# Cross-attention's key stack, written by half of the context: six transfers and two semaphores in place of three transfers and one

## The reference, cut to what matters

```
x   = layernorm(tgt);  self-attention (causal), result = tgt + sa_out
xq  = layernorm(result, ln2)            # 224 rows
xs  = layernorm(src, ln2)               # 750 rows of context
k2, v2 = split(xs @ ed_wkv);  q2 = xq @ ed_wq
wei2 = softmax(q2 @ k2^T * scale)       # per head 224 x 750
result = result + (wei2 @ v2) @ ed_wproj + ed_bproj
result = result + relu(layernorm(tgt, ln3) @ ff_w1 + ff_b1) @ ff_w2 + ff_b2
```

## Time and profile before

| | us |
|---|---|
| median of 3 runs | 1497.84 |
| lowest, highest | 1495.59, 1500.98 |
| the profiled execution's own time | 1497.26 |
| its span, first to last instruction | 1495.4 |
| span of the cross-attention, from 735 on | 760.4 |

### The profile page before, as it was taken

The page is one execution under the profiler, slowest core; times in us unless marked ns, Lnnn a source line. Parts: engine busy times, 40 slices in busy tenths (PEclk is TensorE's granted clock), DMA queues, the critical chain, the costliest instruction groups (busy, mean ns, idle before and its releaser), DMA issues.

```text
span 1495.4 us, 26115 instructions
## 1 busy us (share of the span) xinstructions
PE 1352.8 (90%) x9689; PEld 1113.9 (74%) x9689; DVE 826.8 (55%) x2056; ACT 667.8 (45%) x1622; POOL 654.1 (44%) x547
## 2 busy tenths in 40 slices
PE   6899999995999999998458899999989999999986
PEld 5699988984878888887347676777867677777853
DVE  4421222242477677788325767676675767666551
ACT  4322211241556666565023555463645546374431
POOL 3133322340444555553420455554554445555563
PEclk9999999997999999998768999999999999999996
DMA  5301110034636555654346765566647656665520
GB/s 172 131 22 43 42 42 21 28 129 132 120 68 146 147 131 125 150 122 141 95 80 83 122 89 106 84 103 117 86 91 106 111 85 107 103 94 72 93 36 26
DMA packets 97056, 142.13 MB, mean 95 GB/s; under 512 B 9521, under 2 KB 62553, under 8 KB 95945
## 3 DMA queue, kind: packets, MB, share of 16 engines
q1 hardware_dynamic: 96944, 140.67, 46.8%
HBM read 59.40 MB, written 22.02 MB: 54 GB/s over the span
## 4 chain that ended last, share of the span: by engine, by line
PE 35%; DMA 6%; DVE 4%; ACT 3%; POOL 1%; issue 1%; POOLq 0%; SPq 0%; ACTq 0%
PE ca_ps_acc L1411 16%; PE ca_ps_p L1428 5%; DMA ctx_tokens<-in_ctx_dram 5%; PE ca_ps_s L1441 5%; PE ca_ps_o L1455 5%; PE ca_ps_acc L1504 3%; DVE ca_xT L1394 2%; DVE ca_maxes L1360 1%; ACT ca_f L1329 1%; DMA ca_k_stack<-ca_keys 1%; ACT ca_xT L1323 1%; PE ca_ps_o L1470 1%; POOL ca_partial L1275 1%; ACT ca_probT L1296 1%; PE ca_ps_acc L1496 0%
## 5 line engine op out<-in xcount | busy, mean ns | idle before, releaser
L1275 POOL TENSOR_TENSOR ca_partial<-ca_partial,ca_probT 125x896 f32<-125x896 f32 x128 | 272.5, 2129 | 235.2 <-ACT ca_probT L1296 230.2
L1296 ACT ACTIVATE ca_probT<-ca_ps_p 125x448 f32<-125x448 f32 x384 | 209.8, 551 | 229.7 <-PE ca_ps_p L1428 228.4
L1360 DVE TENSOR_REDUCE ca_maxes<-ca_ps_s 112x1 f32<-112x375 f32 x512 | 253.2, 540 | 84.4 <-PE ca_ps_s L1441 83.8
L1441 PE MATMUL ca_ps_s<-ca_k_stack,ca_q_stack 96*112 96x376 f32 x512 | 173.5, 368 | 34.8 <-DVE ca_maxes L1360 20.8
L1428 PEld LDWEIGHTS ca_ps_p<-ca_q_stack,ca_k_stack 98*125 98x125 f32 x768 | 132.9, 191 | 53.3 <-issue 41.0
L402 PE MATMUL ff_ps_y<-ff_w,ff_hT 128*128 128x512 f32 x672 | 161.0, 396 | 6.7 <-DVE ff_w L63 6.7
L1428 PE MATMUL ca_ps_p<-ca_q_stack,ca_k_stack 98*125 98x224 f32 x768 | 163.4, 297 | 3.2 <-ACT ca_probT L1296 3.0
L1411 PE MATMUL ca_ps_acc<-ca_xT,w_a 128*128 128x376 f32 x768 | 158.9, 345 | 6.7 <-DVE ca_xT L1394 6.7
L262 POOL TENSOR_TENSOR ff_hT<-ff_hrelu,ff_hT 128x256 fp32r<-128x256 f32 x112 | 86.1, 771 | 162.3 <-DVE ff_hT L345 162.3
L1411 PE MATMUL ca_ps_acc<-w_b,ca_xT 128*125 128x512 f32 x576 | 152.5, 401 | 0.8 <-DVE ca_keys L1389 0.8
L402 PEld LDWEIGHTS ff_ps_y<-ff_w,ff_hT 128*128 128x128 f32 x672 | 126.3, 191 | 33.3 <-issue 4.2
(11 more groups left out here) (131 smaller groups left out, 2388.4 us busy)
## 6 DMA issues: line engine op xcount, KB each, us to landing
ca_k_stack<-ca_keys SPq DMA_DIRECT2D x96, 376.0 KB, 8.0
ctx_tokens<-in_ctx_dram SPq DMA_DIRECT2D x8, 1500.0 KB
sa_Q_stack<-sa_rows SPq DMA_DIRECT2D x96, 112.0 KB, 3.4
sa_K_stack<-sa_rows SPq DMA_DIRECT2D x96, 112.0 KB, 3.7
ca_q_stack<-q_out SPq DMA_DIRECT2D x96, 112.0 KB, 10.0
ctx_tokens<-in_L_xattn_ff_w_dram SPq DMA_DIRECT2D x16, 512.0 KB, 4.5
q_out<-sa_yT SPq DMA_DIRECT2D x16, 448.0 KB, 3.6
ff_xin<-in_x_dram SPq DMA_DIRECT2D x7, 512.0 KB, 3.8
```

The lines of the kernel that those rows point to most:

```text
L1275: pool.tensor_tensor(total, total, half(a), ALU.add).then_inc(partial_done, 1)
L1296: act.activation(probT[0:JT, step % PAIRS, u % GH].rearrange("p a t -> p (a t)"), ps_p[u % 2][0:JT, 0:2 * T], ACT.Exp).then_inc(exp_done, 1)
L1360: dve.tensor_reduce(maxes[:, q, j, a:a + 1], ps_s[n % 3][0:TQ, 0:JH], AX_X, ALU.max).then_inc(s_read, 1)
L1441: pe.matmul(ps_s[n % 3][0:TQ, 0:JP], q_stack[0:KS, h, TQ * q:TQ * (q + 1)], k_stack[0:KS, h, a, :], start=True, stop=True).then_inc(s_psum, 1)
```

## The change

The three transfers for a group become six, three for each half `a`. The three of half `a` are issued behind the `K_rest` of that half, and have a semaphore of their own. A piece is then 1,504 bytes, and again there are 128 of them in a transfer; the bytes in all are the same. TensorE waits for half 0 before the first score (which reads half 0) and for half 1 before the second; ACT waits for half `a` of the group before, ahead of writing half `a`. On SP the three transfers of half 0 now stand ahead of `queries` in the steps with `g` = 0, and ahead of `M` in the others.

```diff
-        k_stacked = [sem(f"k_stacked{g}") for g in range(KT)]
+        k_stacked = [[sem(f"k_stacked{g}_{a}") for a in range(2)] for g in range(KT)]
...
-                    if name == "K_rest" and item[2] == 1:
-                        G = item[1]
+                    if name == "K_rest":
+                        _, G, a = item
                         g = G % KT
-                        for a in range(2):
-                            wait_acc_read(sp, place["K", G, a])
+                        wait_acc_read(sp, place["K", G, a])
                         if G >= KT:
                             sp.wait_ge(p_psum, UNITS * (G - KT + 1))
                         for c, half in enumerate(STACK_K):
-                            sp.dma_start(k_stack[HD * c:HD * (c + 1), GH * g:GH * (g + 1)].bitcast(F32),
-                                         keys[:, half].bitcast(F32)).then_inc(k_stacked[g], 16)
+                            sp.dma_start(k_stack[HD * c:HD * (c + 1), GH * g:GH * (g + 1), a].bitcast(F32),
+                                         keys[:, half, a].bitcast(F32)).then_inc(k_stacked[g][a], 16)
...
-                        if a == 0 and G > 0:
-                            act.wait_ge(k_stacked[(G - 1) % KT], STACKED_K * ((G - 1) // KT + 1))
+                        if G > 0:
+                            act.wait_ge(k_stacked[(G - 1) % KT][a], STACKED_K * ((G - 1) // KT + 1))
                         act.copy(keys[:, HI, a], acc[:, 0:JP]).then_inc(khi_done, 1)
...
+                        if u < 2:
+                            pe.wait_ge(k_stacked[G % KT][a], STACKED_K * (G // KT + 1))
                         if u == 0:
-                            pe.wait_ge(k_stacked[G % KT], STACKED_K * (G // KT + 1))
                             pe.wait_ge(q_stacked[G % KT], STACKED_Q * (G // KT + 1))
```

## The result

The changed kernel takes 1526.74 us (median of 4 runs, 1525.16 to 1528.65) against 1499.03 (4 runs, 1495.59 to 1500.98): ratio 1.0188, 95% interval 1.0164 to 1.0211. It is slower by 28 us. The profiled execution took 1528.65 us, with a span of 1526.6, 31.2 us above the span of before. All ratios here are of fast executions; one of six_both_late's ten (1562.51 us) and one of held_both's ten (3283.01 us) were slow and do not enter them.

What follows compares the result with a forecast made beforehand. TensorE's work was taken to set the pace, with the context load's landing the deadline near the change. Profiled 1497.3 - 3 (beginning) + 27.5 (loads) + 9 (clock) = 1530.8, said as 1530 us, 2.2% slower; range 1496 to 1548.

Steps and rivals of the forecast that it cites:

- Fewer waits for the stack: Steady part: TensorE has no stack waits to lose and ACT catches up; 0, bounds 0 and -10.6 us.
- More issues and smaller pieces: SP's 96 more issues and the 1,504-byte pieces, all steps: 0 each; bounds for the issues 0 and +3 us.
- The load with half 0 in its flight: Steps with g = 0: early stack transfers delay the context load, 5 x 5.1 + 2 = 27.5 us, bounds 0 and 38.5.
- The clock: After longer TensorE stops at five loads the granted clock falls to 0.50: 5 x 1.8 = 9 us, bounds 0 and 18.
- The beginning: Phase's beginning: half 0 lands some 3 us earlier and the value product fits in; gain 3 us, bounds 0 and -6.2.
- the bytes to be moved are unchanged, so half 1 lands at about 787 again: Step at the phase's beginning: half 1 lands no sooner than the whole stack did, 787.02; only half 0 gains.
- A: Rival: stack uses the DMA engines the load leaves free, only the beginning's gain is left; 1494 us, chance 0.14.
- B: Rival: as A, and ACT's seven waits, 10.6 us, were passed on to TensorE by the banks; 1484 us, chance 0.11.

Runs made afterwards that it cites:

- six_both_late: Kernel before, with six transfers of 1,504-byte pieces and a semaphore for each half, none issued before both halves are split; 1492.51 us, ratio 0.9954.
- held_both: Changed kernel, but in the six steps with g = 0 and a context load in flight both halves wait for the second; 1496.47 us, ratio 0.9970.

## Why the prediction was right, by its own steps

The forecast was 1530.8 by the sum, 1530 as said, and 1526.74 was measured; the profiled execution, on which the sum was made, took 1528.65.

- *Fewer waits for the stack, 0:* right. Seven waits of ACT went, and the stretches of held_both are those of before.
- *More issues and smaller pieces, 0:* right that they cost nothing, by six_both_late. But they are not neutral at the beginning: there the six transfers bring the whole stack in 2.9 us sooner with nothing issued early.
- *The load with half 0 in its flight, 5.1 us at five places and 2 at the first:* right in mechanism, too large. The load's pieces grew by 4.4 us (15.4 to 19.8), and DVE's waits from 9.8 to 31.6 us over the five, 4.4 each. TensorE stood 21.5 us longer over the five, and the stretch behind the first load grew by 1.3: 22.8 in place of 27.5. The split was 2.5 and 1.9, where I had 3.4 and 1.7. I had taken half 0's price from the beginning of the kernel before, with pieces of double length. With the short pieces the whole stack costs the load 5.2 us there (20.3 in six_both_late against 15.1) and not 6.9, and half of that, 2.6, is close to what half 0 cost.
- *The clock, 1.8 us at five places:* right in mechanism, too small. TensorE's busy time for the same work grew by 13.5 us over the five, where I had 9. Behind the stop at 934 the half clock stood for all or most of 934 to 940, longer than in the one place of before from which I had the 1.8.
- *The beginning, -3:* the mis-sized term of the other sign, -5.9. The stop went down by 4.3 us, not 3, and the stretch up to the next load by another 1.6. The step that failed is "the bytes to be moved are unchanged, so half 1 lands at about 787 again": it was in place 25.4 us after the load's issue, not 28.1, as in six_both_late. Half 0, which I had at 784, was there by 782.39, and what the first score then waited for until 783.76 was the query stack, which I had counted as harmless behind half 0. This new wait, at the one place where the queries are read soon, cost up to 1.4 us.
- *Rivals A and B:* A (the load isn't disturbed) fell with the first load piece of 19 us, and B, whose gain was to come from ACT's seven waits, with the stretches of held_both, 85.3 us without them. The 435 GB/s ceiling that the Trainium skill gives ("DMA: Bandwidth & Descriptors", Specifications) is not contradicted: the wide load reached 258 GB/s. But with load and stack in flight most windows stay well below 200 GB/s, and what the ceiling leaves over did not keep the load from being slowed.

In sum: -5.9 for the beginning, 22.8 for the loads, 13.5 for the clock and 0.9 ahead of the first load make 31.3, against the 31.2 of the spans. The total came out nearer than its terms: the loads were 4.7 us below the forecast and the beginning 2.9, the clock 4.5 above it. That these offset each other in part is luck.

## What to carry to other kernels

Before a transfer is issued earlier, ask what is in flight at that moment and whether the pace hangs on it: here half of a transfer that is read some 21 us later was moved 4.5 us forward, and one with no slack landed 4.4 us later. Two semaphores for two halves can pay even when both halves go out together (1.7 us at the beginning here), and splitting the transfer without moving it was the better form of this change (ratio 0.9954 against 1.0188). Where a load sets the pace, look at its share of the DMA engines first: here a share of 0.32 went with a load that another shape made nearly twice as fast.

## What the runs showed of the hardware that I had not expected

- The shape of this load set its speed: 125 partitions in one transfer ran at 135 GB/s with 0.32 of the DMA engines, 112 and 13 partitions in two at 258 GB/s with 0.92.
- Load and stack, at 135 and 129 GB/s alone, do not add up when both are in flight: at the beginning, after a first window of 194 to 198 GB/s, windows of 2 us show 107 to 124 before (770.9 to 778.9) and 128 to 144 in six_both_late, with the shorter pieces (772.4 to 778.4). Both lose by it. Before, the load took 22.0 us in place of 15.1, and the stack was in place 18.3 us after its issue, where its 1,128 KB would take about 9 at 129 GB/s (an estimate). What they share was not told apart. The stack alone already keeps the share at 1.07, so it also uses the engines that carry the load; that alone could slow the load, and no run tests it.
- The five stops of 5.1 to 6.0 us in the changed kernel cost TensorE 13.5 us of longer busy time besides, 2.7 each, with a granted clock of 0.50 behind the one shown and of 0.96 over each of the four steady stretches. Stops of 1.2 us left the stretch at 1.00. In between both happened: 0.50 after 2.12 and 2.24 us, 1.00 after 2.45.
